# The third layer's experts: hidden features on the partitions, and first weights loaded for each tile

## The chip, the core and the metric

The kernel runs on one core of a Trainium2 chip, in one launch. The metric is the time of the device for one execution, in microseconds, as the median of several runs. Beside the runs there is one profiled execution, from which every row here comes.

## The reference

Four layers, each of a gated cross attention and a gated feed-forward part, on x of 2 x 1024 tokens by 256 features, all in f32. The change concerns only the feed-forward part of the third layer (number 2), a mixture of 8 experts of which each token takes two:

```python
def _L2_ffn_ref(x, Wr, br, W1, b1, W2, b2):          # W1 (8, 256, 512), W2 (8, 512, 256)
    logits = jnp.einsum('btd,de->bte', x, Wr) + br
    topv, topi = jax.lax.top_k(logits, K)              # K = 2
    ...
    gates = jax.nn.softmax(jnp.where(sel_mask, logits, neg_inf), axis=-1)
    h = jax.nn.relu(jnp.einsum('btd,edh->bteh', x, W1) + b1)
    out = jnp.einsum('bte,bteh,ehd->btd', gates, h, W2)
    out = out + jnp.einsum('bte,ed->btd', gates, b2)
    return out
```

x comes in normalised, and the result is added to the running x with a gate.

## The kernel before

The kernel is written engine by engine: each engine has one instruction stream, laid out by hand in Python, and the streams meet at semaphores. There are 8 phases (attention and feed-forward of each layer); phase 5 is the third layer's experts. Matrix products go through two rings of four PSUM banks each, RP and RQ: `take` gives TensorE a bank and waits until the one four places earlier was read, `get` makes a reader wait until the bank is filled.

**Before phase 5.** While phase 4 (attention) ends, the router of the third layer runs in the same streams. For each token it finds two experts, and GpSimd scatters the token's row (256 features and 4 words more) into a table in DRAM, `x2_slots`, at the place of its expert, 32 scatters in all. VectorE then makes a table of tiles (`tile_table`): the slots are cut into NTL = 39 tiles of 128 tokens, each of one expert; `et` holds the expert's number of each tile and `row` its first row in `x2_slots`. `et_made` says that both are there.

**The tiles (phase 5).** `tile_steps` writes out the order of the steps, the same list for TensorE and ScalarE. For each tile i:

- SP loads the tile's 128 rows into one of NXT = 6 buffers `xe`, by the register that it read from `row`. From the seventh tile on it waits until TensorE has turned the tile six back and VectorE has made its destinations.
- "in": TensorE turns the tokens (2 transposes, L1122) so that features lie on partitions, ScalarE copies them to `xeT` (L1397).
- "up": TensorE multiplies with the expert's first weights (L1131). The tokens are the stationary operand (128 x 128), the weights the moving one (512 columns), and the two halves of the 256 features add up: 2 products. The hidden features come out with tokens on partitions. VectorE adds the bias, a row of 512 that stands on all partitions (L2381), and writes `h`.
- "turn": TensorE turns `h` with 4 transposes (L1138), ScalarE applies Relu on the way to `hT` (L1400).
- "down": TensorE multiplies with the second weights, 4 products of 256 columns (L1146), ScalarE scales with the gate weight to `ye` (L1407), and GpSimd scatters the rows to `y2_back` in DRAM (L1661).

Every third tile VectorE works out gate weights and destinations for three tiles (L2300 to L2314), ahead of its bias additions.

The order for TensorE is, once under way: up i, in i+2, turn i-1, down i-2.

**The weights.** The first weights of all 8 experts lie in `W1`, 8192 words a partition at the end of the scratch memory, the second ones in `W2`, 8192 words from word 15000 on. Five experts' first weights fall where phase 4 has nothing, and SP loads them as phase 4 begins (L2488, 512 KB each). The other three, and then all 8 of `W2` (L2498), wait for the last product of phase 4. Behind them SP loads the next attention's weights, waits for the table of tiles and for the scatters, and goes on to the tiles' tokens. TensorE and VectorE read the expert's number of a tile into a register and find weights and bias by it.

**Behind phase 5.** SP waits for the last results' scatters and loads the results, VectorE adds them to x, and phase 6 goes on. TensorE's first work of phase 6 (keys, L669 and L670) needs none of that.

An f32 product shows as two records of TensorE in the trace, each with a weight load (LDWEIGHTS) of its own; a transpose is one record.

Of the kernel before, what the change touches and what calls it, by code (L numbers as in the profile page):

```python
# [137 lines left out]
def build(nc, A, out):  # L138
    ctx = ExitStack()
    with ctx:  # L140
# [80 lines left out]
        kn_made = sem("keys_normalised")  # L221
        kn_clear = sem("key_buffers_cleared")
# [35 lines left out]
        w1_loaded = sem("first_expert2_weights_loaded")  # L258
# [25 lines left out]
        for L in range(4):  # L284
# [180 lines left out]
            if L == 2:  # L465
                v["b1"], v["b2"] = w.take((E2 * H2,)), w.take((D,))
                ld += [(v["b1"], row(A[pre + "b1"].rearrange("e h -> (e h)"), E2 * H2)), (v["b2"][0:E2], A[pre + "b2"])]
# [6 lines left out]
                v["h"] = scratch.take((2, H2))  # L474
# [11 lines left out]

                scratch.at = SA - E2 * DK * H2
                at1 = scratch.at
                v["W1"] = scratch.take((E2 * DK * H2,))
                early = [e for e in range(E2) if at1 + e * DK * H2 >= end16]  # L490
# [125 lines left out]
        def tile_steps():  # L616

            o = [("in", 0), ("in", 1)]
            for i in range(NTL + 2):
                o += [("up", i), ("in", i + 2), ("turn", i - 1), ("down", i - 2)]  # L620
            return [x for n, x in enumerate(o) if 0 <= x[1] < NTL and x not in o[:n]]
# [10 lines left out]
        def _(pe):  # L632
# [479 lines left out]
            def tiled_experts(p):  # L1112
# [3 lines left out]
                for what, i in tile_steps():  # L1116
# [7 lines left out]
                    elif what == "up":  # L1124
                        if i == 0:
                            pe.wait_ge(w1_loaded, 16 * E2)
                        expert[i] = pe.value_load(v["et"][0:1, i:i + 1], min_val=0, max_val=E2 - 1)
                        pe.wait_ge(RP.read, RP.n(p, "in", i))
                        bk = RQ.take(pe, p, "up", i)
                        for k in range(DK):  # L1130
                            last = pe.matmul(bk[:], v["xeT"][:, i % 2, k * P:(k + 1) * P],  # L1131
                                             v["W1"][:, bass.ds(expert[i] * (DK * H2) + k * H2, H2)], start=k == 0, stop=k == DK - 1)
                        last.then_inc(RQ.filled, 1)
                    elif what == "turn":
                        pe.wait_ge(RQ.read, RQ.n(p, "up", i))
                        bk = RP.take(pe, p, "turn", i)
                        for m in range(H2 // P):
                            last = pe.transpose(bk[:, m * P:(m + 1) * P], v["h"][:, i % 2, m * P:(m + 1) * P], ident[:])  # L1138
                        last.then_inc(RP.filled, 1)
                    else:  # L1140
# [1447 lines left out]
```

## Time and profile before

| | |
|---|---|
| median of 3 runs | 1591.49 us (1585.51 to 1594.08) |
| the profiled execution's own time | 1586.5 us |
| its span, first to last instruction | 1584.7 us |
| mean granted clock of TensorE | 0.899 of 2.4 GHz |
| TensorE busy | 1333.0 us, 84% of the span |
| VectorE / ScalarE / GpSimd busy | 713.1 / 478.0 / 303.0 us |
| share of the chain that ended last | TensorE 75%, VectorE 13% |

The span is what the trace covers; the execution's own time is 1.8 us longer. In the rows below PE is TensorE's matmul, PEld its weight load, DVE VectorE, ACT ScalarE, POOL GpSimd and SPq the queue of SyncE, from which most transfers are issued. "L1131" is line 1131 of the kernel. A duration of a PE record reaches over the ones that follow it, since they are pipelined; the chain of waits lays the pieces end to end.

### The profile page before, as it was taken

To read this page: it belongs to the slowest core of one execution; us is meant where nothing else is said; L and a number is where in the kernel's file an instruction comes from. 1 tells how busy PE (TensorE), PEld (TensorE's weight loads), DVE (VectorE), ACT (ScalarE), POOL (GpSimd) and SP (SyncE) were. 2 spreads that over 40 slices of the span, in tenths; PEclk is the share of its full clock that TensorE was granted. 3 is DMA by queue.
4 is the path that set the end of the run, shared out by engine and by line. 5 is a ranking of instruction groups with operands and counts; after the bars stand their busy time and mean duration, and the time that the engine had idled before them with its cause. 6 is when DMAs were issued, how large, how long until landed. Compare 5 with 4: busy or idle time off the path is not lost.

```text
span 1584.7 us, 17797 instructions
## 1 busy us (share of the span) xinstructions
PE 1333.0 (84%) x6201; PEld 783.8 (49%) x6201; DVE 713.1 (45%) x2010; ACT 478.0 (30%) x890; POOL 303.0 (19%) x373
## 2 busy tenths in 40 slices
PE   5999979779998935799887699985778867999997
PEld 2545443334755622464444476753333434666664
DVE  5755253574334289775554322226334445211214
ACT  1244434302122127024342133321543311222220
POOL 5100010041000013330212222232512222122220
PEclk9799989979999968779998699996888787899999
DMA  9990010010000010300003622221000020445425
GB/s 241 257 295 12 1 50 0 0 57 1 0 1 0 1 30 1 120 1 1 25 21 115 182 65 62 63 101 63 1 0 28 28 82 28 149 133 159 151 80 168
DMA packets 93798, 109.90 MB, mean 69 GB/s; under 512 B 10546, under 2 KB 86063, under 8 KB 93583
## 3 DMA queue, kind: packets, MB, share of 16 engines
q1 hardware_dynamic: 86718, 89.87, 19.7%
q0 software_dynamic: 6992, 18.88, 3.3%
q8 instruction: 52, 0.85, 0.2%
q14 instruction: 36, 0.29, 0.1%
HBM read 59.87 MB, written 48.86 MB: 69 GB/s over the span
## 4 chain that ended last, share of the span: by engine, by line
PE 75%; DVE 13%; POOL 4%; issue 3%; ACT 3%; DMA 1%; SPq 1%; DVEq 0%; POOLq 0%; ACTq 0%
PE bank L1097 9%; PE bank L698 5%; PE bank L1131 4%; PE bank L764 4%; PE bank L1179 4%; PE bank L1146 4%; PE bank L784 4%; PE bank L681 4%; PE bank L813 3%; PE bank L955 3%; PE bank L802 3%; PE bank L816 2%; PE bank L639 2%; PE bank L865 2%; PE bank L825 2%
## 5 line engine op out<-in xcount | busy, mean ns | idle before, releaser
L1250 ACT ACTIVATE scratch<-bank 128x512 f32<-128x512 f32 x240 | 126.1, 603 | 108.1 <-PE bank L791 49.9
L1097 PE MATMUL bank<-scratch 128*128 128x320 f32 (+3 forms) x480 | 155.1, 481 | 0.6 <-issue 0.6
L1899 DVE TENSOR_REDUCE scratch<-bank 128x2 f32<-128x308 f32 x256 | 105.8, 472 | 76.0 <-PE bank L764 71.8
L1569 POOL TENSOR_SCALAR rstd<-mv 128x4 f32<-128x4 f32 x36 | 11.0, 306 | 672.3 <-DVE mv L1684 659.0
L1097 PEld LDWEIGHTS bank<-scratch 128*128 128x128 f32 (+1 forms) x480 | 87.8, 186 | 62.3 <-issue 31.4
L1219 ACT ACTIVATE scratch<-bank 128x512 f32<-128x512 f32 x56 | 32.1, 596 | 268.1 <-PE bank L639 257.5
L2396 DVE TENSOR_TENSOR scratch<-scratch,bank 128x320 f32<-128x320 f32 (+3 forms) x60 | 31.4, 526 | 175.9 <-PE bank L1097 169.3
L639 PE MATMUL bank<-ident,scratch 128*128 128x128 f32 x224 | 44.1, 362 | 74.3 <-DVE scratch L1690 74.3
L1598 POOL DMA_INDIRECT x_slots<-scratch x64 | 65.7, 1026 | 138.1 <-DVEq L2257 120.2
L784 PE MATMUL bank<-scratch 32*128 32x512 f32 x384 | 83.8, 669 | 0.0
L764 PE MATMUL bank<-scratch 32*128 32x308 f32 x512 | 82.6, 526 | 1.3 <-DVEq L1763 1.3
L698 PE MATMUL bank<-weights,scratch 128*128 128x256 f32 x320 | 74.7, 389 | 6.3 <-ACT scratch L1314 2.8
L639 PEld LDWEIGHTS bank<-ident,scratch 128*128 128x128 f32 x224 | 36.1, 189 | 88.4 <-DVE scratch L1690 69.8
L2381 DVE TENSOR_TENSOR scratch<-bank,weights 128x512 f32<-128x512 f32 x39 | 27.0, 692 | 115.3 <-PE bank L1131 115.3
L1131 PE MATMUL bank<-scratch 128*128 x156 | 75.4, 606 | 0.4 <-ACT scratch L1397 0.4
L1668 POOL DMA_INDIRECT y_back<-scratch x48 | 45.2, 941 | 158.6 <-ACT scratch L1444 139.3
L1146 PE MATMUL bank<-scratch 128*128 x312 | 73.6, 379 | 0.0
L698 PEld LDWEIGHTS bank<-weights,scratch 128*128 128x128 f32 x320 | 60.7, 194 | 20.1 <-ACT scratch L1314 3.7
L681 PE MATMUL bank<-scratch,weights 128*128 128x512 f32 x128 | 65.8, 667 | 5.6 <-ACT scratch L1219 5.6
L1179 PE MATMUL bank<-scratch 128*128 128x256 f32 (+3 forms) x288 | 68.9, 387 | 0.6 <-DVE scratch L2396 0.6
L764 PEld LDWEIGHTS bank<-scratch 32*128 32x128 f32 x512 | 51.6, 208 | 35.3 <-DVE scratch L1899 11.5
L1661 POOL DMA_INDIRECT y_back<-scratch x39 | 37.4, 959 | 135.4 <-ACT scratch L1407 135.4
(374 smaller groups left out, 2348.8 us busy)
## 6 DMA issues: line engine op xcount, KB each, us to landing
x_slots<-zeros SPq DMA_DIRECT2D x1, 17680.0 KB, 79.6
scratch<-in_L_ffn_W SPq DMA_DIRECT2D x16, 512.0 KB, 8.9
scratch<-y_back SPq DMA_DIRECT2D x16, 512.0 KB, 7.5
scratch<-in_L_ffn_w_gate SPq DMA_DIRECT2D x16, 352.0 KB
scratch<-in_L_ffn_w_up SPq DMA_DIRECT2D x16, 352.0 KB
x_slots<-zeros SPq DMA_DIRECT2D x1, 5200.0 KB, 97.6
scratch<-x_slots SPq DMA_DIRECT2D x39, 130.0 KB, 2.1
y_back<-zeros SPq DMA_DIRECT2D x1, 4352.0 KB, 39.4
```

The source lines that it names most:

```text
L639: last = pe.transpose(bk[:, i * P:(i + 1) * P], v["Y"][:, TPC * c + i, d * P:(d + 1) * P], ident[:])
L681: last = pe.matmul(bk[:], v["Wq"][:, k, m * P:(m + 1) * P], v["yT"][:, k, :], start=k == 0, stop=k == DK - 1)
L698: last = pe.matmul(bk[:, i * D:(i + 1) * D], o[:, tt * P:(tt + 1) * P], v["Wo"][:, m, :], start=m == 0, stop=m == len(rows) - 1)
L764: pe.matmul(bk[:, 0:2 * M], v["QT"][rows, c, m, t * P:(t + 1) * P], v["Kz"][rows, m, b, :, :].rearrange("p e k -> p (e k)"), start=True, s ...
L784: last = pe.matmul(bks[r][:], v["Kz"][rows, m, b, e, 0:P], v["QT"][rows, c, m, :], start=True, stop=not has_max)
L1097: last = pe.matmul(bk[0:fn, 0:n], w[s][:, k, m * P:m * P + fn], moving(k), start=k == 0, stop=k == DK - 1)
L1131: last = pe.matmul(bk[:], v["xeT"][:, i % 2, k * P:(k + 1) * P], v["W1"][:, bass.ds(expert[i] * (DK * H2) + k * H2, H2)], start=k == 0, st ...
L1146: last = pe.matmul(bk[:, 0:D], v["hT"][:, i % 2, m, :], v["W2"][:, bass.ds(expert[i] * (H2 // P * D) + m * D, D)], start=m == 0, stop=m == ...
L1179: last = pe.matmul(bk[0:n, i % 2 * D:(i % 2 + 1) * D], v["hT"][0:fn, e % 2 * 3 + m, i * P:i * P + n], v["Wd"][s][0:fn, m, :], start=m == 0 ...
L1250: act.activation(v["PT"][:, n % 2, j, :], bk[:], ACT.Exp, scale=float(v["hd"]) ** -0.5).then_inc(RP.read, 1)
L1598: pool.indirect_dma_start(x2_slots if L == 2 else x3_slots, bass.IndirectOffsetOnAxis(ap=q["sidx"][:, n:n + 1], axis=0), q["Yx"][:, t, :], ...
L1899: dve.tensor_reduce(v["mx"][:, TPC * c + t, r, 2 * m:2 * m + 2], bk[:, 0:2 * M].rearrange("p (e k) -> p e k", k=M), AX.X, ALU.max)\
```

## The change

The first product swaps its operands: the weights are stationary (128 x 128) and the tokens move (128 columns), 4 x 2 products of 128 columns. The hidden features come out with features on partitions, as the second product needs them, and the turning of `h` goes. VectorE adds a bias that now has one value for each partition and block of features, and ScalarE applies Relu from `h` to `hT` (semaphore `hidden_made`).

The weights' addresses no longer hang on the expert: `W1` is three buffers of one expert's weights, right behind `W2`, and SP loads them tile by tile, with the expert's number in a register. All eight loads of first weights during phase 4 go; the first three tiles' come after the table of tiles and ahead of the wait for the scatters. The bias is loaded as 8 x 4 columns of 128 values, instead of a row of 4096 on each partition.

The order for TensorE becomes: up i, in i+2, down i-1.

```diff
@@ -255,7 +256,7 @@
         yb_loaded = [sem(f"results_loaded_{c}") for c in range(4)]
         EWN = 4
         ew_loaded = [sem(f"expert3_loaded_{i}") for i in range(3)]
-        w1_loaded = sem("first_expert2_weights_loaded")
+        w1_loaded = [sem(f"first_expert2_weights_loaded_{i}") for i in range(3)]
         w2_loaded = sem("second_expert2_weights_loaded")
         et_made = sem("experts_of_tiles_made")
         NXT = 6
@@ -463,15 +464,15 @@
                 v["ohb"] = scratch.take((NT, E), BF16)
                 v["ohs"] = scratch.take((NT + 1, E), BF16)
             if L == 2:
-                v["b1"], v["b2"] = w.take((E2 * H2,)), w.take((D,))
-                ld += [(v["b1"], row(A[pre + "b1"].rearrange("e h -> (e h)"), E2 * H2)), (v["b2"][0:E2], A[pre + "b2"])]
+                v["b1"], v["b2"] = w.take((E2 * (H2 // P),)), w.take((D,))
+                ld += [(v["b1"], col(A[pre + "b1"].rearrange("e h -> (e h)"), E2 * H2 // P)), (v["b2"][0:E2], A[pre + "b2"])]
                 v["G"] = scratch.take((NT, E))
                 v["GT"] = scratch.take((2, CH))
                 assert scratch.at <= ROUTING[2]
                 scratch.at = ROUTING[2]
                 v["xe"] = scratch.take((NXT, YW))
                 v["xeT"] = scratch.take((2, DK * P))
-                v["h"] = scratch.take((2, H2))
+                v["h"] = scratch.take((2, H2 // P, P))
                 v["hT"] = scratch.take((2, H2 // P, P))
                 v["ye"] = scratch.take((3, D))
                 v["til"], v["run"] = scratch.take((4 + E,)), scratch.take((2, 4 + E))
@@ -483,11 +484,8 @@
                 assert scratch.at <= EXPERTS
                 scratch.at = EXPERTS
                 v["W2"] = scratch.take((E2 * (H2 // P) * D,))
-
-                scratch.at = SA - E2 * DK * H2
-                at1 = scratch.at
-                v["W1"] = scratch.take((E2 * DK * H2,))
-                early = [e for e in range(E2) if at1 + e * DK * H2 >= end16]
+                v["W1"] = scratch.take((3, DK, H2))
+                assert scratch.at <= SA
                 scratch.at = NT * YW
                 v["yk"] = scratch.take((NT, D))
             if L == 3:
@@ -617,7 +615,7 @@
 
             o = [("in", 0), ("in", 1)]
             for i in range(NTL + 2):
-                o += [("up", i), ("in", i + 2), ("turn", i - 1), ("down", i - 2)]
+                o += [("up", i), ("turn", i - 1), ("in", i + 2), ("down", i - 1)]
             return [x for n, x in enumerate(o) if 0 <= x[1] < NTL and x not in o[:n]]
 
         def turned(p, c, d):
@@ -1122,25 +1120,19 @@
                             last = pe.transpose(bk[:, d * P:(d + 1) * P], v["xe"][:, i % NXT, d * P:(d + 1) * P], ident[:])
                         last.then_inc(RP.filled, 1)
                     elif what == "up":
-                        if i == 0:
-                            pe.wait_ge(w1_loaded, 16 * E2)
                         expert[i] = pe.value_load(v["et"][0:1, i:i + 1], min_val=0, max_val=E2 - 1)
+                        pe.wait_ge(w1_loaded[i % 3], 16 * (i // 3 + 1))
                         pe.wait_ge(RP.read, RP.n(p, "in", i))
                         bk = RQ.take(pe, p, "up", i)
-                        for k in range(DK):
-                            last = pe.matmul(bk[:], v["xeT"][:, i % 2, k * P:(k + 1) * P],
-                                             v["W1"][:, bass.ds(expert[i] * (DK * H2) + k * H2, H2)], start=k == 0, stop=k == DK - 1)
+                        for m in range(H2 // P):
+                            for k in range(DK):
+                                last = pe.matmul(bk[:, m * P:(m + 1) * P], v["W1"][:, i % 3, k, m * P:(m + 1) * P],
+                                                 v["xeT"][:, i % 2, k * P:(k + 1) * P], start=k == 0, stop=k == DK - 1)
                         last.then_inc(RQ.filled, 1)
-                    elif what == "turn":
-                        pe.wait_ge(RQ.read, RQ.n(p, "up", i))
-                        bk = RP.take(pe, p, "turn", i)
-                        for m in range(H2 // P):
-                            last = pe.transpose(bk[:, m * P:(m + 1) * P], v["h"][:, i % 2, m * P:(m + 1) * P], ident[:])
-                        last.then_inc(RP.filled, 1)
-                    else:
+                    elif what == "down":
                         if i == 0:
                             pe.wait_ge(w2_loaded, 16 * E2)
-                        pe.wait_ge(RP.read, RP.n(p, "turn", i))
+                        pe.wait_ge(hidden_made, i + 1)
                         bk = RP.take(pe, p, "down", i)
                         for m in range(H2 // P):
                             last = pe.matmul(bk[:, 0:D], v["hT"][:, i % 2, m, :],
@@ -1396,8 +1388,8 @@
                         bk = RP.get(act, p, "in", i)
                         act.activation(v["xeT"][:, i % 2, :], bk[:, 0:D], ACT.Copy).then_inc(RP.read, 1)
                     elif what == "turn":
-                        bk = RP.get(act, p, "turn", i)
-                        act.activation(v["hT"][:, i % 2], bk[:].rearrange("p (m t) -> p m t", t=P), ACT.Relu).then_inc(RP.read, 1)
+                        act.wait_ge(RQ.read, RQ.n(p, "up", i))
+                        act.activation(v["hT"][:, i % 2], v["h"][:, i % 2], ACT.Relu).then_inc(hidden_made, 1)
                     elif what == "down":
                         if i >= 3:
 
@@ -2378,7 +2370,11 @@
                                      v["xe"][:, s:s + 3, D:YW], spare2[:, cols], v["etf"][:, cols], True)
                     e = dve.value_load(v["et"][0:1, i:i + 1], min_val=0, max_val=E2 - 1)
                     bk = RQ.get(dve, p, "up", i)
-                    dve.tensor_tensor(v["h"][:, i % 2, :], bk[:], v["b1"][:, bass.ds(e * H2, H2)], ALU.add).then_inc(RQ.read, 1)
+                    if i >= 2:
+                        dve.wait_ge(hidden_made, i - 1)
+                    dve.tensor_tensor(v["h"][:, i % 2], bk[:].rearrange("p (m t) -> p m t", t=P),
+                                      bc(v["b1"][:, bass.ds(e * (H2 // P), H2 // P)].unsqueeze(2), (P, H2 // P, P)), ALU.add)\
+                       .then_inc(RQ.read, 1)
 
             def expert_out(p, e, c, gate_of):
                 for q in range(2):
@@ -2482,17 +2478,8 @@
                     q = ph[5]
                     pre = "L2_ffn_"
 
-                    def first_weights(es):
-                        for e in es:
-                            n = DK * H2
-                            sp.dma_start(q["W1"][:, e * n:(e + 1) * n].rearrange("p (k h) -> p k h", k=DK), kin(A[pre + "W1"][e]))\
-                              .then_inc(w1_loaded, 16)
-
-                    sp.wait_ge(phase_over, 4)
-                    first_weights(early)
 
                     sp.wait_ge(RQ.filled, RQ.n(4, "out", NC - 1, 1))
-                    first_weights([e for e in range(E2) if e not in early])
                     for e in range(E2):
                         n = H2 // P * D
                         sp.dma_start(q["W2"][:, e * n:(e + 1) * n].rearrange("p (m d) -> p m d", d=D),
@@ -2508,10 +2495,26 @@
                         r = sp.value_load(v["row"][0:1, i:i + 1], min_val=0, max_val=XT2 - P)
                         sp.dma_start(v["xe"][:, i % NXT, :], x2_slots[bass.ds(r, P), :]).then_inc(xt_loaded[i % NXT], 16)
 
+                    w1 = A[pre + "W1"].rearrange("e k n -> (e k) n")
+
+                    def first_weights(i):
+                        if i >= 3:
+                            sp.wait_ge(RQ.filled, RQ.n(p, "up", i - 3))
+                        e = sp.value_load(v["et"][0:1, i:i + 1], min_val=0, max_val=E2 - 1)
+                        sp.dma_start(v["W1"][:, i % 3], w1[bass.ds(e * D, D), :].rearrange("(k p) n -> p k n", p=P))\
+                          .then_inc(w1_loaded[i % 3], 16)
+
                     sp.wait_ge(et_made, 1)
+                    for i in range(3):
+                        first_weights(i)
                     sp.wait_ge(scattered, 16 * 2 * NT)
+                    for i in range(NXT):
+                        tile_tokens(i)
                     for i in range(NTL):
-                        tile_tokens(i)
+                        if i + NXT < NTL:
+                            tile_tokens(i + NXT)
+                        if i + 3 < NTL:
+                            first_weights(i + 3)
                     for i in range(3):
                         sp.wait_ge(yt_back[i], 16 * len(range(i, NTL, 3)))
                     results(v, y2_back, FAR2)
```

## Rows read from the trace of the kernel before

**Rows 1.** Windows: busy time of each engine, granted clock (PEclk), DMA

```profile
core 0: us, PE busy (x) PEld busy (x) DVE busy (x) ACT busy (x) POOL busy (x), PEclk, DMA share, GB/s
849.90:851.50 1.60, 1.60 (x18) 1.60 (x17) 0.68 (x2) 0.26 (x1) 0.00 (x0) 1.00 0.00 0
...
905.00:1045.00 140.00, 140.00 (x617) 98.72 (x616) 34.37 (x125) 49.42 (x102) 32.60 (x34) 1.00 0.20 61
```

**Rows 2.** Groups by line and shape, 893 to 1060 us

```profile
L1131 PE MATMUL bank<-scratch 128*128 x156 | 75.4, 606 | 0.4 <-ACT scratch L1397 0.4
...
L2381 DVE TENSOR_TENSOR scratch<-bank,weights 128x512 f32<-128x512 f32 x39 | 27.0, 692 | 115.3 <-PE bank L1131 115.3
...
L1400 ACT ACTIVATE scratch<-bank 128x512 f32<-128x512 f32 x39 | 23.3, 597 | 5.1 <-PE bank L1138 3.2
```

**Rows 3.** Chain of waits, one tile: start us, us, what

```profile
971.50 1.72 PE bank L1131 x4
973.21 0.22 PE bank L1122 x2
973.43 0.44 PE bank L1138 x4
973.87 1.73 PE bank L1146 x8
975.60 1.72 PE bank L1131 x4
```

**Rows 4.** Chain of waits, end of the stage

```profile
1053.51 3.46 PE bank L1146 x16
1056.97 0.43 PE bank L669 x2
```

**Rows 5.** Chain of waits, the router's product

```profile
850.02 1.69 PE bank L1056 x16
```

**Rows 6.** Timeline of TensorE there: start us, us, engine line operation, shape

```profile
849.86 1.85 PE L1056 MATMUL bank<-weights,scratch 128*128 128x8 f32 x16
```

**Rows 7.** Timeline, VectorE: addition, and last instruction of the destinations

```profile
977.47 0.69 DVE L2381 TENSOR_TENSOR scratch<-bank,weights 128x512 f32<-128x512 f32 x1 [3.41 <-PE bank L1131]
...
979.08 0.17 DVE L2314 CAST scratch<-scratch 128x3 uint32<-128x3 f32 x1
```

**Rows 8.** Timeline, SP's queue: two token loads, one behind the other

```profile
891.84 0.34 SPq L2509 DMA_DIRECT2D scratch<-x_slots  x1
...
892.95 0.34 SPq L2509 DMA_DIRECT2D scratch<-x_slots  x1
```

**Rows 9.** Source view of L2488, eight loads of 512 KB; ns min/median/max

```profile
L2488 SPq DMA_DIRECT2D scratch<-in_L_ffn_W x8: 368/482/1453, 653.9 to 859.6; - x8
...
DMA to landing us min/median/max: 3.9/8.9/11.6
```

**Rows 10.** DMA issues, 858 to 858.9 us: KB each, us to landing

```profile
scratch<-in_L_ffn_W SPq DMA_DIRECT2D x1, 512.0 KB, 3.9
```

**Rows 11.** Windows: head of the stage, and the last layer's experts

```profile
880.00:885.00 5.00, 2.81 (x8) 1.83 (x9) 1.42 (x4) 0.59 (x1) 3.80 (x4) 0.50 1.07 243
...
895.00:900.00 5.00, 4.92 (x8) 2.37 (x9) 1.74 (x9) 0.45 (x2) 0.00 (x0) 0.56 0.50 117
...
1401.00:1413.00 12.00, 12.00 (x50) 7.99 (x49) 2.42 (x11) 3.60 (x9) 2.82 (x3) 1.00 0.45 148
```

**Rows 12.** Chain of waits, head of the stage

```profile
885.02 4.63 DMA x_slots<-scratch
```

**Rows 13.** Timeline, VectorE: last instruction of the table of tiles

```profile
879.35 0.30 DVE L2293 CAST scratch<-scratch 128x39 uint32<-128x39 f32 x1
```

**Rows 14.** DMA issue of the second layer's bias, timeline of third's bias and router

```profile
weights<-in_L_ffn_b SPq DMA_DIRECT2D x1, 4.0 KB, 7.2
...
653.02 0.81 SPq L2454 DMA_DIRECT2D weights<-in_L_ffn_b  x2
...
768.67 1.85 PE L1056 MATMUL bank<-weights,scratch 128*128 128x8 f32 x16
```

More of the change, by code:

```diff
@@ L221, in build @@
         kn_made = sem("keys_normalised")
+        hidden_made = sem("hidden_features_made")
         kn_clear = sem("key_buffers_cleared")
```

## Prediction

> **What bounds the kernel now.** I read the windows of the stage first. From 905 to 1045 us TensorE is busy for all 140 us at a granted clock of 1.00 (the upper level, 2.4 GHz), VectorE for 34 and ScalarE for 49, and the DMA engines have a share of 0.20 [rows 1]. So the tiles of the third layer's experts are bound by TensorE, and only what changes in its stream of instructions, or makes it wait, changes the time. The groups by shape say what that stream is [rows 2], but their durations overlap (a product of 592 ns starts every 430), so for prices I take the chain of waits [rows 3], where the pieces lie end to end: one tile is 1.72 us of first product (L1131, 4 records), 0.22 of turning a later tile's tokens (L1122, 2 records), 0.44 of turning the hidden features (L1138, 4 records) and 1.73 of second product (L1146, 8 records). Together 4.10 us, and the next L1131 starts 4.10 us after the last. 39 tiles of it are 160 us of the 1584.7. At the end of the stage the next layer's keys (L669) start on TensorE in the moment in which the last L1146 ends [rows 4], and the results' way back hangs on the last tile too, so a shorter stage moves everything behind it forward.
>
> **What is removed: the turning.** Four transposes for each tile, with nothing of them hidden: 39 x 0.44 = **-17.2 us** [rows 3].
>
> **What is changed: the first product.** Before, 2 products of 512 columns, each as two records, so 4 records of 0.43 us. After, 8 products of 128 columns, again two records each, so 16 records. The streamed columns are the same (4 x 512 = 16 x 128), a quarter of 0.43 = 0.107 us for each record, 1.72 us in all. What grows is the number of weight loads, 4 to 16. The question is what a record with a weight load of its own and only 128 columns costs. No f32 product of that size runs at the full clock in this trace, so I bound it:
> - Weight loads alone: the router's product (L1056) loads 128x128 f32 for 8 columns, 16 times in 1.69 us [rows 5], shape in [rows 6], at clock 1.00 [rows 1]. That is 0.106 us for each, nearly all of it the load.
> - Loads beside a stream: L1146 streams 256 columns with a load each and takes 1.73 / 8 = 0.216 us a record; half of L1131's 0.43 would be 0.215 [rows 3]. So its load of 0.106 lies wholly beside the stream.
> - Both at the size wanted: a transpose has a load of 128 columns and a stream of 128, and takes 0.44 / 4 = 0.110 us [rows 3]. Its load is shorter as an instruction than a product's, so it is a near row and no proof.
>
> From below the price is 16 x 0.106 = 1.70 us a tile, from its nearest neighbour 16 x 0.110 = 1.76, and from above, load and stream one after the other, 16 x (0.106 + 0.107) = 3.41. L1146 speaks for overlap, so I take 1.74, +0.02 a tile, 39 x 0.02 = **+0.8 us**. The far end stays as a rival.
>
> The 0.106 us of L1146's hidden load also bears on a rule. The Trainium skill, "TensorE: Matmul & The Clock Gate", section "The mechanism", says that a weight load overlaps a matmul in flight only when the two use different row groups. All loads here use all 128 rows, so by that rule each record would pay load and stream, the rival of 3.41 us. The trace disagrees at 256 columns (0.216 us, not 0.32); no row here decides it at 128.
>
> **What is added on ScalarE and VectorE.** VectorE's bias addition keeps its 512 elements (692 ns before, L2381) and ScalarE's Relu too (597 ns, L1400), which now reads what VectorE wrote [rows 2]. Hidden: their busy time is 34 and 49 of 140 us. The new chain is first product, VectorE 0.69, ScalarE 0.60, second product. The addition starts 0.15 us after the product's end (977.47 [rows 7] against 975.60 + 1.72 = 977.32 [rows 3]), so with two handovers of some 0.1 it is 1.7 us. Between the end of tile i's first product and its second stand turning (0.22), the second product of i-1 (1.73) and the first of i+1 with another turning (1.96): 3.9 us. Covered. What stands behind ScalarE's new wait is its copy of tile i+2's tokens, which TensorE needs a whole tile later, and covered likewise. At the last tile only the second product of tile 37 (1.73) covers the 1.7: I count +0.1. The two pieces of 1.73 at the end stay [rows 4].
>
> **What is moved: the first weights.** They come per tile, 39 x 512 KB instead of 8 x 512 KB, into three buffers. SP's loop has, for each tile, a token load and a weight load. A token load with its register read takes 1.11 us, 0.34 of it the issue [rows 8]; so a weight load, with the 0.48 us of such an issue [rows 9], is 0.77 + 0.48 = 1.25 us and both 2.36, below a tile's 3.69. SP's loop waits for VectorE's destinations once in three tiles; these end at 979.25, 1.94 us after the first product [rows 7], and 1.94 + 1.11 is still below 3.69.
>
> Load i+3 starts when first product i is done. It reads the expert's number (0.8 us with the wake-up), and a load of 512 KB on idle queues lands 3.9 us after its issue [rows 10]: 4.7 us. Needed at the start of first product i+3: 3 x 3.69 - 1.74 = 9.3 us. Margin 4.6 us, cost 0. The queues aren't idle, but nearly: 61 GB/s at share 0.20 [rows 1] and 512 KB each 3.69 us (142 GB/s) make some 210 GB/s; the last layer's experts run with 148 GB/s at share 0.45, TensorE busy all 12 of 12 us beside it [rows 11], which by proportion is a share of 0.64.
>
> **The head of the stage.** The late weights before were 3 of the first product and 8 of the second, and they filled the DMA engines to 885 us [rows 11]. After, 8 come there, and 3 come once the experts' numbers and rows of the tiles are made (879.65 us [rows 13]), in all the same 11. They now run beside the last scatter of tokens, which lands 4.63 us after its issue and opens the stage [rows 12]. The three may delay it by what they hold, at most 3 x 0.52 MB at the 243 GB/s of this window, 6.5 us; but as the backlog is lower by the same, I count 0. TensorE's granted clock at its first tile is 0.56 [rows 11], half speed; that stays.
>
> **The bias.** It was 2 MB in rows and becomes 4096 single elements. The second layer's bias, 1024 single elements, lands in 7.2 us [rows 14], so by four times that (an estimate) this one in some 30 us. It is issued at 653 us and used at the router's first product at 768 [rows 14]: hidden by 115 us, and the rest of the time it would cost in full. Behind it in SP's queue stands only the wait for the attention's last product.
>
> **Sum.** -17.2 + 0.8 + 0.1 = **-16.3 us**. Against the profiled execution's own 1586.5 us: 1570.2. The median of the runs shown is 5.0 above that execution, 1591.5, so 1575.2; I say **1575**.
>
> **Rivals.**
> - *Load and stream in series* (the side of slower). Place: the 16 records of the first product. 3.41 - 1.72 - 0.44 = +1.25 us a tile, 39 x 1.25 = +49: 1640 us. It loses from 0.135 us a record on ((1.72 + 0.44) / 16). Against it is L1146; for it, that 128 columns leave only 0.001 us between load and stream, so any cost of switching shows. Chance 0.06; another 0.05 for a part of it, 0.115 to 0.135 us, gain 3 to 15 us.
> - *The weights come late.* The ring's round is 0.8 + landing + 1.74, for three tiles. It binds from a landing of 8.5 us, and loses from 9.8 (3 x 4.10 - 2.54). In a queue of several such loads the landing was 8.9 in the median and 11.6 at worst [rows 9]; with 8.9 a tile takes 3.81, and 39 x -0.29 = -11: 1580. With 11.6 it takes 4.71, +24: 1615. For it: each load waits behind tokens and results; against: one load at a time, share 0.64. Chance 0.12, a third of it slower.
> - *The head slips.* The scatter lands up to 6.5 us later, or the first product waits for its three loads: -10, 1582. Chance 0.08.
> - *It doesn't do what it says:* TensorE's gap stays, since something else ends at 4.10 us a tile, SP's loop or the VectorE chain above mis-sized: no change, 1591. Chance 0.05.
>
> **How the numbers follow.** Forecast, as summed, -20 to -13: chance 0.64, own range 1570 to 1582 with the spread of medians. Half a per cent is 8 us, about what the measurement tells from no change. Faster: 0.64, 0.03 of the partial series, 0.07 of the late weights, 0.05 of the head, 0.79 less 0.03 for a median of three runs that spread over 8.6 us: 0.76. Slower: 0.06, 0.04 of the late weights, 0.01 of the head: 0.11. Same: 0.13. The range goes from 1567 to 1592, which takes in the head, no change and late weights at the median, and leaves out series, the worst landing and the outer runs, some 0.15.
>
> **What would show it.** The first product as 16 records in 1.70 to 1.76 us at clock 1.00, no transposes but L1122's, a tile in 3.67 to 3.71 us, the stage's end near 1040.7 instead of 1057.0. Wrong: gaps before the first product released by a DMA (late weights), records of 0.2 us (series), a first tile after 897 (head), gaps before the second product (VectorE and ScalarE).

## The result, and the profile after

In the five runs of each that came with the result the kernel before takes 1592.3 us in the median and the changed one 1581.1: 11.2 us less. The ratio estimated from all these runs is 0.9917, 95% interval 0.9890 to 0.9945, which is 13 us of 1592, with an interval from 9 to 17.5. Forecast were 16.3 us less and a time of 1575 us, in a range from 1567 to 1592. A repetition on another chip gave 0.9952 (below). The single runs of either kernel spread over 9 to 10 us, which is nearly the size of the change, so the trace says more about it than the times.

The windows of the changed kernel, in the middle of the stage:

```profile
core 0: us, PE busy (x) PEld busy (x) DVE busy (x) ACT busy (x) POOL busy (x), PEclk, DMA share, GB/s
915.00:1045.00 130.00, 130.00 (x907) 122.78 (x906) 35.66 (x131) 47.94 (x105) 32.78 (x36) 1.00 0.68 207
```

Against [rows 1] TensorE is busy all the time as before, at the same clock. Its weight loads fill 122.8 of 130 us (before 98.7 of 140), and the DMA engines' share went from 0.20 to 0.68. The chain of waits, one tile:

```profile
962.01 1.78 PE bank L1129 x16
963.79 0.22 PE bank L1120 x2
964.01 1.73 PE bank L1138 x8
965.74 1.78 PE bank L1129 x16
```

L1129 is the first product, L1120 the tokens' turning, L1138 the second product. The 0.44 us of [rows 3] are gone, the first product went from 1.72 to 1.78, and a tile from 4.10 to 3.73 us: 39 x 0.37 = 14.4 us. Nothing waits for a DMA in the middle of the stage.

The chain at the head of the stage, against [rows 11, 12]:

```profile
894.98 4.96 DMA x_slots<-scratch
...
901.79 2.06 DMA scratch<-x_slots
...
904.87 3.75 PE bank L1129 x16
908.63 0.43 PE bank L1120 x2
909.05 2.50 PE bank L1129 x16
```

The last scatter lands 4.96 us after its issue, before 4.63. The second tile's product takes 2.50 us: TensorE's granted clock is 0.72 in the mean over these 2.50 us and 0.50 over the 4 us before, so for a part of it TensorE is at its lower level (1.2 instead of 2.4 GHz). And at the end, against [rows 4]:

```profile
1049.40 1.74 PE bank L1138 x8
...
1051.25 0.47 ACT scratch L1399
1051.73 0.53 ACT scratch L1392
1052.25 0.14 issue
1052.40 1.99 PE bank L1138 x8
1054.38 0.43 PE bank L667 x2
```

Here is something that wasn't forecast. In the kernel before, the last two second products ran as one piece of 3.46 us. Now TensorE stands for 1.27 us between them: it waits for ScalarE's Relu of tile 38 (L1392), and that began only when ScalarE was done with scaling tile 37 (L1399).

I call "the stage" the time from the first record of the first product to the first of the next layer's keys. It was 1056.97 - 895.08 = 161.9 us and is 1054.38 - 904.87 = 149.5, so **12.4 us** shorter. But the profiled executions differ by 2.6 us only (spans 1584.7 and 1582.1): the changed one reaches the stage 9.8 us later. Behind the stage both take 527.7 us. Of the 9.8 us, 4.1 are there already at SP's load of the router's bias, as phase 4 begins; ahead of it the change alters no instruction but for addresses. The timelines of SP's queue, before and then changed:

```profile
652.51 0.47 SPq L2454 DMA_DIRECT2D weights<-in_L_ffn_br  x1
```

```profile
656.59 0.47 SPq L2450 DMA_DIRECT2D weights<-in_L_ffn_br  x1
```

### The profile page after: what moved, and what is told of

Read it like the earlier page. It is cut to its first block, busy times and chain, and to the rows that moved or that the text cites. A ratio compares the mean times of both kernels' runs of the same rounds, so it can differ in the third digit from the quotient of the medians.

```text
span 1582.1 us, 18540 instructions
## 1 busy us (share of the span) xinstructions
PE 1323.3 (84%) x6487; PEld 814.7 (51%) x6513; DVE 712.8 (45%) x2010; ACT 475.4 (30%) x890; POOL 302.8 (19%) x373
## 4 chain that ended last, share of the span: by engine, by line
PE 75%; DVE 13%; POOL 4%; issue 3%; ACT 3%; DMA 1%; SPq 0%; DVEq 0%; POOLq 0%; ACTq 0%
PE bank L1095 9%; PE bank L696 5%; PE bank L1129 5%; PE bank L762 4%; PE bank L1171 4%; PE bank L782 4%; PE bank L1138 4%; PE bank L679 4%; PE bank L811 3%; PE bank L800 3%; PE bank L953 3%; PE bank L637 2%; PE bank L814 2%; PE bank L863 2%; PE bank L823 2%
## 5 line engine op out<-in xcount | busy, mean ns | idle before, releaser
L696 PE MATMUL bank<-weights,scratch 128*128 128x256 f32 x320 | 78.8, 405 | 6.2 <-ACT scratch L1306 2.7
L1129 PEld LDWEIGHTS bank<-scratch 128*128 128x128 f32 x624 | 78.1, 197 | 2.6 <-issue 0.7
L1129 PE MATMUL bank<-scratch 128*128 128x128 f32 x624 | 78.5, 281 | 0.3 <-issue 0.3
L1660 POOL DMA_INDIRECT y_back<-scratch x48 | 45.2, 941 | 158.4 <-ACT scratch L1436 139.1
L1138 PE MATMUL bank<-scratch 128*128 x312 | 73.9, 380 | 1.3 <-ACT scratch L1392 1.3
```

Of the source, the lines that this page charges most:

```text
L696: last = pe.matmul(bk[:, i * D:(i + 1) * D], o[:, tt * P:(tt + 1) * P], v["Wo"][:, m, :], start=m == 0, stop=m == len(rows) - 1)
L1129: last = pe.matmul(bk[:, m * P:(m + 1) * P], v["W1"][:, i % 3, k, m * P:(m + 1) * P], v["xeT"][:, i % 2, k * P:(k + 1) * P], start=k == 0, ...
L1138: last = pe.matmul(bk[:, 0:D], v["hT"][:, i % 2, m, :], v["W2"][:, bass.ds(expert[i] * (H2 // P * D) + m * D, D)], start=m == 0, stop=m == ...
```

## The experiments

Stages and tiles, all read from the chains of waits as above (from the first product's start to the keys' start), ratios to the kernel before on the same chip:

| run | tile, us | first product, us | stage, us | starts at, us | ratio (95%) |
|---|---|---|---|---|---|
| before | 4.10 | 1.72 | 161.9 | 895.1 | |
| changed | 3.73 | 1.78 | 149.5 | 904.9 | 0.9917 (0.9890 to 0.9945) |
| Relu first | 3.73 | 1.78 | 147.2 | 903.3 | 0.9893 (0.9867 to 0.9920) |
| weights resident | 3.73 | 1.78 | 149.6 | 903.5 | 0.9905 (0.9870 to 0.9939) |
| old product, weights per tile | 4.10 | 1.72 | 161.8 | 898.1 | 0.9991 (0.9976 to 1.0007) |
| extra turning | 4.17 | 1.78 | 164.2 | 904.4 | 1.0017 (0.9999 to 1.0036) |
| changed, again | 3.73 | 1.78 | 148.7 | 907.4 | 0.9952 (0.9935 to 0.9969) |
| before, again | 4.10 | 1.72 | 162.6 | 905.9 | |
| interleaved | 3.73 | 4 x 0.445 | 147.9 | 901.3 | 0.9938 (0.9920 to 0.9957) |
| 64 columns | 3.69 | 1.73 | 149.4 | 905.8 | one run, 1584.8 us |
| 96 columns | 3.71 | 1.76 | 148.5 | 904.0 | one run, 1583.1 us |
| one buffer | 6.9 | 2.07 | 269.0 | 907.8 | one run, 1702.9 us |
| two buffers | 3.73 | 1.78 | 150.8 | 899.1 | one run, 1579.3 us |

The first four experiments ran on one chip, the next three rows on another. The last four rows are single executions on a third chip, where the one execution of the kernel before took 1594.5 us; single executions spread by some 10 us, so small differences between these four are read from the traces alone.

**The gap at the end.** In ScalarE's stream the Relu of the last tile changes places with the scaling before it:

```diff
+                o = tile_steps()
+                a, b = o.index(("down", NTL - 2)), o.index(("turn", NTL - 1))
+                o[a], o[b] = o[b], o[a]
-                for what, i in tile_steps():
+                for what, i in o:
```

> The changed kernel, with one swap in ScalarE's order: the Relu of the last tile (38) stands before the scaling of tile 37's second product, not behind it. Theory A (the 1.27 us of TensorE's gap before the last second product is ScalarE's own order: scaling 37 must wait for second product 37, and the Relu stands behind it): the Relu runs right after VectorE's addition, at 1.1 us after the end of the last first product, the gap falls from 1.27 us to under 0.1, and the stage from the first L1129 to the first product of the next attention's keys falls from 149.5 to 148.0 us. Theory B (the gap is the length of the chain addition, Relu, handovers, 3.0 us against a cover of 1.73): the swap changes nothing, the gap stays at 1.2 us or more. In total time 1.4 us is too little to be told; both give 0.990 to 0.992 of the time of before.

```profile
1045.01 1.78 PE bank L1129 x16
1046.80 3.65 PE bank L1138 x16
1050.45 0.43 PE bank L667 x2
```

The gap of 1.27 us is gone from the chain of this run's end: the two second products are one piece of 3.65 us, where the kernel before had 3.46. So the gap was ScalarE's order (A), not the length of the chain (B). In the timeline the Relu starts 0.89 us after the end of the last first product:

```profile
1047.68 0.63 ACT L1395 ACTIVATE scratch<-scratch 128x512 f32<-128x512 f32 x1 [1.55 <-DVE scratch L2378]
```

The stage is 2.3 us shorter than the changed kernel's. The tail accounts for 1.33 (from 1049.40 to 1054.38 there, 4.98 us, against 3.65); the rest is the head, where TensorE reached its full clock earlier (the second tile's product took 1.79 instead of 2.50 us). That I count as chance, since nothing there was changed.

**The weights' way.** All eight experts' first weights resident, as before, with the new product. Each tile takes a fixed expert's weights and not its own, so the values of this layer's experts are others:

```diff
-                                last = pe.matmul(bk[:, m * P:(m + 1) * P], v["W1"][:, i % 3, k, m * P:(m + 1) * P],
+                                last = pe.matmul(bk[:, m * P:(m + 1) * P], v["W1"][:, (i * E2 // NTL) * (DK * H2) + k * H2 + m * P:(i * E2 // NTL) * (DK * H2) + k * H2 + (m + 1) * P],
```

> The new first product and no turning, as in the changed kernel, but all eight experts' first weights resident as in the kernel before, five loaded as the attention begins and three after it. A tile takes its weights from a fixed expert (tile number times 8 over 39) and not from its own, so the values of the third layer's experts are others. It leaves out the 39 loads in the stage. Theory A (loads per tile are hidden): a tile stays at 3.73 us, 1.78 of it the first product, and the stage at 149 to 150 us. Theory B (the loads' traffic, 207 GB/s at share 0.68, slows TensorE's reads, and the record of 0.111 us instead of 0.107 is that): the first product falls to 1.72 us and the tile to 3.67, the stage by 2.3 us. Theory C (the loads delay the head): the first L1129 starts up to 1 us earlier behind the last scatter's issue.

The windows of this run:

```profile
915.00:1045.00 130.00, 130.00 (x908) 122.83 (x907) 35.03 (x130) 47.82 (x104) 33.59 (x35) 1.00 0.22 66
```

66 GB/s instead of 207, and a tile takes 3.73 us, 1.78 of them the first product, to the hundredth as with the loads; the stage 149.6. A holds; B falls: the traffic isn't what makes a record 0.111 us. C falls too: from the last scatter's issue to the first product it is 12.2 us here (891.31 to 903.46) and 9.9 in the changed kernel, so later and not earlier. In the two profiles of the kernel before it is 10.1 and 10.2 us.

The other way round, the old product and turning with three buffers and a load for each tile, SP's part as in the change:

```diff
-                                             v["W1"][:, bass.ds(expert[i] * (DK * H2) + k * H2, H2)],
+                                             v["W1"][:, i % 3, k, :],
```

> The kernel before, product and turning as they were, with only the weights changed: three buffers, loaded for each tile by the expert's number, the first three behind the table of tiles. Theory A (hidden): a tile stays at 4.10 us and the stage at 161.9 us, the time within 0.3% of before. Theory B (the loads cost something of their own): a tile over 4.10 us, or gaps before the first product that a DMA ends, and a time above that of before by what they add.

```profile
915.00:1045.00 130.00, 130.00 (x572) 91.75 (x571) 32.39 (x120) 46.51 (x96) 29.74 (x31) 1.00 0.64 190
```

The loads make 190 GB/s, and TensorE is busy all the time at a granted clock of 1.00. Tile 4.10, stage 161.8, ratio 0.9991 (0.9976 to 1.0007): A. The loads per tile cost nothing that can be told, neither alone nor with the new product.

**The turning put back.** The two transposes of the tokens are made three times, four of the six for nobody:

```diff
+                        for d in range(DK):
+                            last = pe.transpose(bk[:, D + d * P:D + (d + 1) * P], v["xe"][:, i % NXT, d * P:(d + 1) * P], ident[:])
+                        for d in range(DK):
+                            last = pe.transpose(bk[:, D + d * P:D + (d + 1) * P], v["xe"][:, i % NXT, d * P:(d + 1) * P], ident[:])
                         last.then_inc(RP.filled, 1)
```

> The changed kernel with four more transposes a tile (the tokens' two, twice again, into a free half of the same bank; nobody reads them), so the number of transposes is that of before. Theory A (the gain is the turning, at 0.109 us each): a tile takes 3.73 + 0.44 = 4.17 us, 0.07 above the 4.10 of before, the stage is 166 to 167 us, 4 to 5 above that of before, and the time 1.000 to 1.005 of it. Theory B (part of the gain is that the second product waits for less): a tile stays under 4.10 us and the time clearly below that of before.

```profile
962.47 1.78 PE bank L1133 x16
964.26 0.22 PE bank L1120 x2
964.48 0.22 PE bank L1122 x2
964.69 0.22 PE bank L1124 x2
964.91 1.73 PE bank L1142 x8
966.64 1.78 PE bank L1133 x16
```

A tile takes 4.17 us, as expected, and the ratio is 1.0017 (0.9999 to 1.0036). With as many transposes as before, nothing is left of the gain: the turning is all of it (A). The stage, 164.2, missed the 166 to 167 expected, by its head: the extra turning of the first two tiles lies ahead of the first product, and the full clock came earlier (the second tile's product took 1.79 us instead of 2.50).

**What a record costs.** The first product with fewer columns of tokens (64 and 96 of 128):

```diff
-                                last = pe.matmul(bk[:, m * P:(m + 1) * P], v["W1"][:, i % 3, k, m * P:(m + 1) * P],
-                                                 v["xeT"][:, i % 2, k * P:(k + 1) * P], start=k == 0, stop=k == DK - 1)
+                                last = pe.matmul(bk[:, m * P:m * P + 64], v["W1"][:, i % 3, k, m * P:(m + 1) * P],
+                                                 v["xeT"][:, i % 2, k * P:k * P + 64], start=k == 0, stop=k == DK - 1)
```

> The changed kernel, but the first product streams only the first 64 of the 128 tokens of each of its 8 products (the other 64 are left out, so the values of the third layer's experts are others). Weight loads as before, 16 a tile. Theory A (a record takes the longer of load and stream, 0.106 and 0.107, and 0.004 for their tie): 0.106 us a record, first product 1.69 us, tile 3.64. Theory B (the record pays the load and a share of its stream, since the router's product with 8 columns took 0.1056 and this one with 128 takes 0.111): 0.108 us, 1.73, tile 3.68. Theory C (load and stream in series): 0.053 less than with 128, 0.058 us, 0.93.

> As the run with 64 columns, with 96 of 128 tokens in each product, 32 left out. Theory A (the longer of the two): 0.106 us a record, 1.69 us a tile, so that the step to 0.111 comes only at 128. Theory B (a share of the stream): 0.1096 us, 1.75. Theory C (series): 0.085 us, 1.35.

The chains, with 64 and then with 96 columns:

```profile
963.92 1.73 PE bank L1129 x16
965.65 0.23 PE bank L1120 x2
965.88 1.73 PE bank L1138 x8
967.61 1.73 PE bank L1129 x16
```

```profile
964.41 1.76 PE bank L1129 x16
966.16 0.22 PE bank L1120 x2
966.38 1.73 PE bank L1138 x8
```

1.73, 1.76 and 1.78 us for 64, 96 and 128 columns: 0.108, 0.110 and 0.111 a record, and the router's with 8 columns took 0.106 [rows 5]. B's numbers came, A's and C's didn't. Half the columns save 3% of the product. So what a record pays whatever its columns, some 0.106 us, sets the pace, and the stream adds a few ns. That this fixed part is the weight load is argued and not shown: a transpose's load takes 0.14 us as an instruction and a product's 0.19, and yet their records take 0.109 and 0.111 us. Why the stream adds its few ns these runs don't show either.

**How long a load takes.** One buffer and two in place of three (the threes that belong to the first weights become R):

```diff
-                v["W1"] = scratch.take((3, DK, H2))
+                v["W1"] = scratch.take((R, DK, H2))
...
-                        if i >= 3:
-                            sp.wait_ge(RQ.filled, RQ.n(p, "up", i - 3))
+                        if i >= R:
+                            sp.wait_ge(RQ.filled, RQ.n(p, "up", i - R))
```

> The changed kernel with one buffer for the first weights in place of three, so each load starts when the first product of the tile before has ended, and the next first product waits for it. This shows the landing of a load in the stage. Theory A (queues nearly idle, 3.9 us and a little): a tile takes 0.8 + 4.4 + 1.78 = 7.0 us, with a gap of some 3.3 us before each first product that a DMA ends. Theory B (the traffic makes a load late, 7.5 us as the result loads or more): a tile takes 10 us or more, and three buffers were near their limit.

> The changed kernel with two buffers for the first weights. The round is 0.8 + landing + 1.78 for two tiles. Theory A (landing 4.4): 7.0 / 2 = 3.5, below a tile's 3.73: nothing changes, stage 149 to 150 us. Theory B (landing over 4.9): a tile over 3.73, at a landing of 7.5 it takes 5.0 us and the stage some 200 us.

The chain with one buffer:

```profile
960.72 3.69 DMA scratch<-in_L_ffn_W
964.41 0.04 issue
964.46 2.07 PE bank L1129 x16
...
967.27 3.63 DMA scratch<-in_L_ffn_W
970.90 0.04 issue
```

A load lands 3.7 us after its issue (3.6 to 4.0 in the 38 of the stage), and from one to the next it is 6.55 us here, 6.9 in the mean (7.0 expected); the execution takes 1702.9 us. The mean is above the 6.55 mainly because in some tiles TensorE, which now stands still for a part of each, is at its lower level: from 970.94 to 974.48 us its granted clock is 0.56, and this first product takes 3.54 us. All this is with half the traffic (114 GB/s), so it isn't yet the landing under full traffic. Two buffers show that: a round has room for a landing of 4.9 us, a tile stays at 3.73, and the waits of TensorE's matmuls between 905 and 1045 us that a load ends are 1.5 us in two places:

```profile
PE bank L1129 <- DMA scratch<-in_L_ffn_W: 1.5, 2, 0.9
```

Its weight loads wait in four places, 2.8 us in all. So at 203 GB/s a load lands within 4.9 us nearly always, where three buffers leave room for 8.6. A in both, though with two buffers the stage takes 150.8 us where A said 149 to 150: 1.5 us are these waits.

**Where the stage begins, and both products interleaved.** The last three runs shared a chip: the changed kernel and the one before once more, and a version in which one second product (of tile i-2) follows each two first products (`second(i, m)` is product m of tile i's four):

```diff
-                o += [("up", i), ("turn", i - 1), ("in", i + 2), ("down", i - 1)]
+                o += [("up", i), ("turn", i - 1), ("down", i - 2), ("in", i + 2)]
...
                         for m in range(H2 // P):
                             for k in range(DK):
...
+                            second(i - 2, m)
```

> The changed kernel once more, for its ratio and for a second profile. In the first profile the stage was 12.4 us shorter than before, but it began 9.8 us later (904.87 against 895.08 us), because TensorE's granted clock was lower in stretches of the attention ahead of it (0.93 and 0.94 where before had 1.00). Theory A (that is chance between executions, since before's own runs lie between 1585.5 and 1595.6): the ratio is 0.990 to 0.993 and the stage 149 to 150 us, wherever it begins. Theory B (the change itself brings the later start): the stage begins at 903 us or later again in every profile of a kernel with the new product, while one of the kernel before stays near 895.

> The kernel before once more, for a second profile of where its stage begins. Theory A (chance): the first L1131 starts anywhere from 895 to 905 us. Theory B (the change brings it): it starts at 895 to 898 us again. The stage is 161.7 us in both.

> The changed kernel with the second product one tile later and interleaved with the first: after each two first products of tile i (128 columns) comes one second product of tile i-2 (256 columns). Theory A (the first product's 16 records are paced by their weight loads of 0.108 us, ahead of 0.107 of stream; a load beside a stream of 0.213 has time to spare): the 24 records take less than 1.78 + 1.73 = 3.51 us, down to 3.41 by the streams alone, a tile 3.63 to 3.70 instead of 3.73; the second products at the end follow one another without the gap of 1.27 us, and the stage falls from 149.4 to 145 to 147.5 us, the time by 2 to 4 us. Theory B (each change of operand or bank costs, or the dynamic addresses of the second product stall the sequencer): a tile over 3.73 and the stage 149 us or more.

The kernel before reached its first product at 905.87 us this time, 10.8 later than in its first profile:

```profile
905.87 3.77 PE bank L1131 x4
```

So a late start comes without the change too, and B falls as it was put (the interleaved kernel began at 901.3 us, the one with two buffers at 899.1). That the change has no part in it isn't shown. From SP's load of the router's bias to the first product, the ten profiles with the new product take 246.8 to 250.0 us, and the three with the old one 242.6, 242.7 and 248.0. If the change adds something here, the bias is left to carry it, since "weights resident" (248.2) differs from the kernel before in nothing else ahead of the stage; no run tests this.

The windows of the stretch from 794 to 821 us, in this second profile of before,

```profile
794.00:821.00 27.00, 23.86 (x146) 13.87 (x140) 14.24 (x36) 9.41 (x18) 4.11 (x5) 0.91 0.06 20
```

have TensorE's granted clock at 0.91, where the first profile has 1.00 from 792 to 842 us. The changed kernel's first profile has 0.93 there.

The repetition's ratio is 0.9952 (0.9935 to 0.9969), outside the 0.990 to 0.993 of A. The stage is 148.7 against 162.6 us, 13.9 shorter, but the medians differ by 8.1 only (1585.4 against 1593.5). The changed kernel's eight runs have a mean granted clock of 0.889 to 0.895, those of before 0.895 to 0.898. Taking 12.4 us at full clock out of the runs of before would leave 0.8955. So by this estimate, in these runs the changed kernel lost some 4 us (12.4 less 8.1) to the lower level somewhere outside the stage. Whether that is chance or comes with the change stays open: in the first five runs, with mean clocks of 0.892 to 0.901, the medians are 11.2 us apart.

Interleaving did nothing for the product: four chunks of 0.445 us, 1.78 in all, and a tile of 3.73.

```profile
911.53 0.22 PE bank L1134 x2
911.75 0.45 PE bank L1143 x4
912.20 0.43 PE bank L1122 x2
912.63 0.45 PE bank L1143 x4
```

L1143 is the first product here, L1122 the second. So a weight load that has the longer stream of the second product beside it makes the chunk no faster, and my theory of pacing by the loads alone (A) falls here, as it fell at 96 columns. The gap at the end went with it; the last 18 records of the second product are one piece:

```profile
1045.31 3.89 PE bank L1122 x18
```

The stage is 147.9 us, where A said 145 to 147.5.

## Why the prediction was right, and where it was off

The time of 1581.1 us lies in the range, but a kernel without any gain (1591) would have lain between 1567 and 1592 too, so the time alone says little; the account rests on the stage in the trace. There the gain, 12.4 us, is short of the 16.3 summed and just outside the -20 to -13 of "as summed".

- **What bounds the stage**: right. But for the 1.27 us at its end TensorE stayed busy, and the stage's length followed its stream.
- **The turning, -17.2 us**: right, shown by putting it back (4.17 us a tile, gain gone).
- **The first product, +0.8 us**: the mechanism right (loads beside the streams, 0.111 us a record against 0.107 by the stream and 0.213 in series), the size short: 1.78 us where I took 1.74, so 39 x 0.06 = 2.3 us. The 1.76 that I gave "from its nearest neighbour", the transpose's 0.110, would have been the better price, though the transpose's load is shorter as an instruction, so that the two agree may be chance. The tile came out at 3.73 us, just outside my 3.67 to 3.71.
- **The rule of the Trainium skill** ("TensorE: Matmul & The Clock Gate", section "The mechanism") that a load overlaps a matmul only in another row group: now the trace disagrees at 128 columns too, 1.78 us and not 3.41. I had left out that the same section also lets a load go ahead of a running matmul when it goes to the background weight buffer; this trace doesn't contradict that.
- **The chain over ScalarE, +0.1 us**: this step failed. I wrote that "at the last tile only the second product of tile 37 (1.73) covers the 1.7". But in ScalarE's order the last Relu stands behind the scaling of that very second product. It can't lie beside it and starts after it. In the order before, with the second product two tiles behind the first, the last Relu stood ahead of that scaling; the new order of steps turned the two around. The end took 4.98 us instead of 3.46, 1.27 of it the gap: +1.5. I had listed what stands behind ScalarE's new wait and not what the Relu now stands behind.
- **The loads per tile, 0**: right, in both directions. Share 0.68 for my 0.64, 207 GB/s for some 210, landing 3.7 us for 3.9.
- **The head, 0**: right. The sign that I gave for a slipping head, a first tile after 897 us, did come (904.9), but not from the head: the last scatter landed 0.33 us later, and from its issue to the first product it is 9.9 us against 10.1 before. The start is late by what was lost ahead of the router and in the attention, where the granted clock was lower in stretches. The second tile's product lay between 1.78 and 2.57 us in profiles of both kernels, by the moment at which the clock rose: up to 0.8 us either way.
- **The bias, 0**: no engine waits for a DMA between 600 and 900 us. The 30 us that I gave its load were far too long: it is issued at 657.10 us, and from 665 us on the DMA engines' share is 0.01. SP's issue of the two bias loads takes 3.38 us instead of 0.81, though, and whether the bias moves the start of the stage is open (above).

The sum of the stage with the measured sizes: -17.2 + 2.3 + 1.5 = -13.4, and +0.7 for the second tile's product at the lower clock (2.50 us against 1.84), -12.7; measured -12.4. The medians are 11.2 us apart in the first runs (13 by the ratio) and 8.1 on another chip. The rivals "in series", "late" and "doesn't do what it says" are excluded by the tile of 3.73 us.

The version with the Relu first has the lowest ratio of those that ran: 0.9893 (0.9867 to 0.9920) of before, with a stage 2.3 us shorter than the changed kernel's. The two weren't timed on the same chip, and their intervals overlap.

## What to carry to other kernels

When an engine is full for a whole stage, the pieces of its chain of waits price a stretch well: the tile came out within about 1% (3.73 us for 3.69). The gain is a small difference of such sums and was off by a quarter (12.4 us for 16.3), so the ends of the stage are worth a sum of their own. Transfers that got a deadline of their own cost nothing here as long as their round (issue, landing, use) was shorter than the buffers allow; take that sum first. Where the order of steps changes, look at what each instruction now stands behind in its engine's order, at the last tile above all, where the cover of the next tile is missing. And when a change is of the size by which single runs spread, measure the stage in several profiles.

## What the runs showed of the hardware

- An f32 record of TensorE with a load of 128x128 of its own takes 0.106 us with 8 columns, 0.108 with 64, 0.110 with 96, 0.111 with 128 and 0.216 with 256, at clock 1.00. So halving the columns from 128 gains nearly nothing.
- The first product doesn't feel the DMA engines: 207 and 66 GB/s beside it give the same 1.78 us.
- A load of 512 KB landed 3.6 to 4.0 us after its issue beside 114 GB/s, and nearly always within 4.9 beside 203 GB/s.
- The granted clock took different courses in two executions of one program: the same instruction came 10.8 us later in the second. With TensorE standing still for a part of each tile (one buffer) the granted clock was 0.95 in the mean of the stage, against 1.00 in the full stage from 915 to 1045 us.
